# Two seams of a macaron block (FFN, attention, FFN): a low part ahead of the stage's last scaling, back-transposes behind two value units, and a last group finished and stored in halves

## The reference

```
x = x + 0.5 * ffn(layernorm(x))
x = x + attention(layernorm(x))      # q, k of width 16, v of width 64, 16 heads
x = x + 0.5 * ffn(layernorm(x))
```

## Time and profile before

| | us |
|---|---|
| median of 3 runs | 790.72 (789.14 to 791.90) |
| the profiled execution, its own time | 790.52 |
| its span, first to last instruction | 788.70 |
| PE busy, share of the span | 774.3, 98% |
| DVE busy, share of the span | 675.9, 86% |
| ACT busy, share of the span | 616.1, 78% |

### The profile page before, as it was taken

How to read it: one execution, slowest core, us unless ns; L and a number is a source line. 1 busy time by engine, 2 the same in 40 slices (tenths; PEclk the granted TensorE clock), 3 DMA queues, 4 the chain that set the end, 5 groups by cost and what they waited for, 6 DMA issues and landing times.

```text
span 788.7 us, 11788 instructions
## 1 busy us (share of the span) xinstructions
PE 774.3 (98%) x3638; PEld 467.5 (59%) x3638; DVE 675.9 (86%) x1347; ACT 616.1 (78%) x1018; POOL 201.6 (26%) x262
## 2 busy tenths in 40 slices
PE   8989999999999999999999999999999899999998
PEld 5868888888773333333333332333498678888886
DVE  6888878889869999999999999999547888878786
ACT  3867766766668999999999999999616676777763
POOL 3115633334301111111111112111112037333331
PEclk8999999999999999999999999999999999999999
DMA  6041312110274111111311111110000123202111
GB/s 178 1 164 53 108 54 107 53 54 1 107 289 139 54 54 53 55 54 54 107 54 54 54 54 54 54 54 1 2 1 1 48 117 141 73 20 87 54 53 54
DMA packets 25413, 54.65 MB, mean 69 GB/s; under 512 B 5264, under 2 KB 10768, under 8 KB 23312
## 3 DMA queue, kind: packets, MB, share of 16 engines
q1 hardware_dynamic: 25360, 54.00, 20.0%
HBM read 44.42 MB, written 9.57 MB: 68 GB/s over the span
## 4 chain that ended last, share of the span: by engine, by line
PE 90%; DVE 5%; ACT 2%; DMA 2%; issue 1%; SPq 0%; POOL 0%; DVEq 0%; ACTq 0%
PE ps L932 29%; PE ps L920 11%; PE ps L368 7%; PE ps L379 7%; PE ps L370 7%; PE ps L369 7%; PE ps L380 7%; PE ps L381 7%; PE ps L939 4%; ACT ef L1009 1%; PE ps L350 1%; DMA w2raw<-in_w 1%; DVE hlo L645 1%; PE ps L200 1%; DMA xt<-in_x 1%
## 5 line engine op out<-in xcount | busy, mean ns | idle before, releaser
L1073 DVE TENSOR_SCALAR_CACHE_REDUCE ef<-ps 128x1024 f32<-128x1024 f32 x256 | 307.2, 1214 | 6.6 <-PE ps L920 0.2
L1009 ACT ACTIVATE ef<-ef,nmax 128x1024 f32<-128x1024 f32 x256 | 293.9, 1149 | 8.9 <-DVE ef L1073 2.3
L932 PE MATMUL ps<-ef,vs 128*64 128x512 f32 x1024 | 247.9, 605 | 0.2
L454 ACT ACTIVATE ps<-ps,b_sb 128x512 f32<-128x512 f32 x256 | 169.0, 663 | 94.9 <-PE ps L370 92.9
L645 DVE TENSOR_TENSOR hlo<-ps,hhi 128x512 fp32r<-128x512 f32 x256 | 165.4, 685 | 4.5 <-ACT ps L454 0.2
L932 PEld LDWEIGHTS ps<-ef,vs 128*64 128x64 f32 x1024 | 62.7, 136 | 120.5 <-issue 108.2
L641 DVE CAST hhi<-ps 128x512 fp32r<-128x512 f32 x128 | 87.6, 684 | 54.2 <-ACT ps L454 54.1
L1117 POOL TENSOR_TENSOR vs<-V,rsum 128x128 f32<-128x128 f32 x128 | 51.3, 401 | 294.1 <-DVE rsum L1079 294.1
L501 POOL TENSOR_TENSOR acc<-acc,ysc 128x512 f32<-128x512 f32 x55 | 70.7, 1289 | 150.7 <-DVE ysc L668 150.1
L368 PE MATMUL ps<-xhi,w1lo 128*128 128x512 f32 x256 | 102.6, 401 | 0.4 <-DVE hlo L645 0.3
L379 PE MATMUL ps<-hhi,w2lo 128*128 128x512 f32 x256 | 101.5, 397 | 0.9 <-DVE gT L716 0.9
(11 more groups left out here) (98 smaller groups left out, 675.0 us busy)
## 6 DMA issues: line engine op xcount, KB each, us to landing
gb<-gates SPq DMA_DIRECT2D x16, 1024.0 KB, 4.6
qs<-qk_parts SPq DMA_DIRECT2D x32, 256.0 KB, 3.3
ks<-qk_parts SPq DMA_DIRECT2D x32, 256.0 KB, 3.9
w1raw<-in_w SPq DMA_DIRECT2D x16, 256.0 KB, 4.9
w2raw<-in_w SPq DMA_DIRECT2D x16, 256.0 KB, 5.6
qk_parts<-sthi SPq DMA_DIRECT2D x16, 256.0 KB, 2.3
qk_parts<-stlo SPq DMA_DIRECT2D x16, 256.0 KB, 2.9
xt<-in_x SPq DMA_DIRECT2D x4, 256.0 KB, 4.3
```

The source lines that it names most:

```text
L454: nc.scalar.activation(bank(mc), bank(mc), ACT.Gelu, bias=b1_sb[:, u, mc:mc + 1]).then_inc(F.gelu, 1)
L932: last = nc.tensor.matmul(bank(6 + half)[x * VD:(x + 1) * VD, :], vs[:, t % VRING, x * VD:(x + 1) * VD], ef[:, (2 * t + x) % ERING, half * ...
L1009: nc.scalar.activation(ef[:, c, :], ef[:, c, :], ACT.Exp, scale=-1.0, bias=nmax[:, c:c + 1], accum_out=esum[:, c:c + 1]).then_inc(s_exp, 1)
L1073: nc.vector.tensor_scalar(ef[:, c, :], bank(slot_bank(u), 2), -1.0, None, ALU.mult, ALU.min, accum_out=nmax[:, c:c + 1]).then_inc(s_max, 1)
```

## The change

At the first seam, VectorE runs `low_dve` of group 0 before the scaling of stage 7 and no longer after it. TensorE runs `back_pe` of group 3 after `values(0)` and `values(1)` and no longer between `queries(0)` and `values(0)`; `values(0)`, which writes bank 7, waits for one scaling fewer (that of stage 6, which reads this bank).

At the end, the scaling of the last stage is two instructions of 256 columns, each with a semaphore of its own; `finish_pe` writes tiles 0 and 1 to bank 1 and tiles 2 and 3 to bank 2 and waits for each half; the residual of group 3 is two instructions of 256 columns; and its store is two DMAs of 128 KB. VectorE's order there is both halves of the scaling, the residual of group 2, both halves of the last residual. Three semaphores are added.

```diff
+        def finish_bank(t):
+            return bank((1, 2)[t // 2])[:, t * P:(t + 1) * P]
+
         def finish_pe(pe, n, g):
             F = ffns[1]
             pe.wait_ge(F.acc, A0 + GR * (E - 3) + g + 1)
...
+            for half in range(2):
+                for t in range(2 * half, 2 * half + 2):
+                    at = (g * TPG + t) * P
+                    nc.tensor.matmul(finish_bank(t), acc[:, at:at + P], ident, start=True, stop=False)
+                    if t == 0:
+                        pe.wait_ge(s_part, 1)
+                    if t == 2:
+                        pe.wait_ge(F.scaled, S0 + GR * E)
+                    last = nc.tensor.matmul(finish_bank(t), ysc[:, (2 * GR - 1) % 2, t * P:(t + 1) * P],
+                                            ident, start=False, stop=True)
+                last.then_inc(s_fin, 1)
+
+        def last_scaled_dve(dve):
+            F, s = ffns[1], 2 * GR - 1
+            dve.wait_ge(F.y, (E // 2 - 1) * 2 * GR + (s + 1 + Y0))
+            dve.wait_ge(F.acc, (E // 2 - 1) * 2 * GR + (s + A0 - 1 - GR))
+            for half in range(2):
+                part = slice(half * 256, half * 256 + 256)
+                at = (GR - 1) * 512 + half * 256
+                nc.vector.scalar_tensor_tensor(ysc[:, s % 2, part], bank(Y_BANKS[s % 4])[:, part], b2_sb[:, E - 1:E],
+                                               gb[:, 1, at:at + 256], ALU.add,
+                                               ALU.mult).then_inc((s_part, F.scaled)[half], 1)
+
+        def last_residual_dve(dve, n):
+            g = GR - 1
+            for half in range(2):
+                dve.wait_ge(s_fin, half + 1)
+                at = g * TPG + 2 * half
+                xg = xt[:, at:at + 2, :]
+                src = bank((1, 2)[half])[:, half * 256:half * 256 + 256].rearrange("p (t d) -> p t d", d=D)
+                nc.vector.tensor_tensor(xg, xg, src, ALU.add).then_inc(s_last, 1)
...
+                residual_dve(dve, m, 1)
                 if m.k == 1:
-                    residual_dve(dve, m, 1)
+                    low_dve(dve, m, 0)
                     back(i, 7)
-                    low_dve(dve, m, 0)
                     statistics_dve(dve, m, 1)
                 else:
-                    residual_dve(dve, m, 1)
-                    back(i, 7)
+                    last_scaled_dve(dve)
                     residual_dve(dve, m, 2)
-                    residual_dve(dve, m, 3)
+                    last_residual_dve(dve, m)
...
                 if unit == 0:
-                    pe.wait_ge(ffns[0].scaled, S0 + GR * E)
+                    pe.wait_ge(ffns[0].scaled, S0 + GR * E - 1)
...
             queries(0)
-            back_pe(pe, n, 3)
             values(0)
             values(1)
+            back_pe(pe, n, 3)
...
-            for g in range(GR):
+            for g in range(GR - 1):
                 sp.wait_ge(norms[3].res, g + 1)
                 sp.dma_start(out_v[g], xt[:, g * TPG:(g + 1) * TPG, :]).then_inc(s_out, 16)
-            sp.wait_ge(s_out, 16 * GR)
+            for half in range(2):
+                sp.wait_ge(s_last, half + 1)
+                at = (GR - 1) * TPG + 2 * half
+                sp.dma_start(out_v[GR - 1][:, 2 * half:2 * half + 2, :], xt[:, at:at + 2, :]).then_inc(s_out, 16)
+            sp.wait_ge(s_out, 16 * (GR + 1))
```

More of the change, by code:

```diff
@@ L136, in macaron_kernel @@
         s_out = sem("s_out")
+        s_part = sem("s_part")
+        s_fin = sem("s_fin")
+        s_last = sem("s_last")
         class Norm:
```

## The result

The changed kernel has a median of 787.54 us in 22 runs (785.96 to 793.31), the kernel before 790.91 us in 22 runs (787.87 to 795.90); the ratio is 0.9958, with a 95% interval of 0.9942 to 0.9975. The profiled execution of the changed kernel took 788.84 us, its span is 787.0, with the same mean granted clock as the profiled one of before, 0.993: 1.7 us shorter. The mean granted clock is TensorE's, as a share of full speed over the whole execution. These two numbers, 3.4 us between the medians and 1.7 us between two executions at one clock, are what had to be explained.

What follows compares the result with a forecast made beforehand. TensorE held 90% of the chain that ended last, so only places where the chain leaves it could save. First seam 0.49 plus end 0.97 made 1.46 us, taking 790.72 to 789.3 us (0.18%), range 788.2 to 790.9.

Steps and rivals of the forecast that it cites:

- The seam's step of 0.49 us: First seam: TensorE starts 1.26 us early, but VectorE's chain lets 0.49 us remain; bounds 0 and 1.26.
- predicted wait of 1.0 to 1.4 us: First seam: TensorE's wait ahead of `forward_pe` of group 2 grows from 0.57 to about 1.3 us.
- The half instructions: End: a scaling of 256 columns takes 0.48 us, a residual of 256 columns 0.41 us.
- The end, put at 0.97: End: 0.97 us earlier, from 0.56 by the engines and 0.46 by the half store, less 0.05 lost.
- the prediction's own signs of being wrong: First scores not 0.49 us earlier, attention of another length, or span's end still 2.67 us behind the last issue.
- How the numbers follow: Prediction's section on cases and range: forecast 0.60, likeliest 789.3 us, range 788.2 to 790.9, within 0.3% at 0.86.
- the moved back-transposes: First seam: `back_pe` of group 3 comes at 204.6, after GpSimd's addition ending at 204.40, so no wait; no gain stated.
- The seam gives nothing: Rival, chance 0.15: another wait, nearest the keys' landing before the first scores, takes the first seam's gain; 789.75 us.
- The stores don't overlap: Rival, chance 0.05: at the end each store waits for the one before to land; slower, 792.0 us.
- The end gives little: Rival, chance 0.12: half instructions cost nearly the whole, or last byte's receipt doesn't follow the size; 789.9 us.
- the half store: End: the last store of 128 KB saves 0.46 us by the rows; the skill's rate gives an estimated 0.30.
- All of the lead stays: Rival, chance 0.06: first seam keeps all 1.26 us of TensorE's lead; with the end 2.2 us, 788.5 us.

Runs made afterwards that it cites:

- the low part alone: Kernel before with only the swap putting `low_dve` of group 0 ahead of the scaling: 792.72 us, ratio 0.9997; again 792.61 us, 0.9998.
- e11_change_third: The changed kernel run a third time, no edit, against the kernel before in the same rounds: median 788.44 us, ratio 0.9969.
- e2_change_again: The changed kernel run once more, no edit, against the kernel before in the same rounds: median 791.20 us, ratio 0.9981.
- e15_change_fourth: The changed kernel run again in later rounds, no edit, against the kernel before: median 789.56 us, ratio 0.9982.
- the seam alone: Kernel before with only the first seam's edits (low part, back-transposes, one scaling fewer to wait for): median 788.95 us, ratio 0.9978.
- the end alone: The changed kernel with the first seam's edits taken out, against the kernel before: median 789.96 us, ratio 0.9969.
- the filled kernel: Kernel before plus five matmuls that nothing reads, ahead of the first query unit at the first seam; first set 790.42 us, ratio 0.9977.

## Why the prediction came out as it did

**The sum held in its steps.** It said 1.46 us; at equal clock it is 1.65 (intervals 1.47 to 1.85 and 1.49 to 1.79 for the first set and the later three, 1.52 to 1.78 for all). The traces add up to 0.50 us to the first scores and 0.94 at the end, 1.44; the 0.2 us between that and the fit aren't explained. The low part at VectorE's idle time, no wait of `queries(0)`, `rstd` behind GpSimd's addition: each is in the trace where it was put. The seam's step of 0.49 us measured 0.54 at the forward transposes, and of TensorE's predicted wait of 1.0 to 1.4 us there 0.83 came at the transposes and 0.56 at `queries(3)`, which the prediction had named. The half instructions, put at 0.48 and 0.41 us, are 0.478 and 0.422. The end, put at 0.97, is 0.94 and 0.95 in traces and 1.06 (0.82 to 1.30) at equal clock. Of the prediction's own signs of being wrong, one showed in the profiled execution: the first scores came 0.33 us earlier and not 0.49, as the keys were waited for; over the traces of either kind it is 0.50.

**The step that failed is the one from the sum to the median**, in "How the numbers follow": "The runs spread over 789.14 to 791.90, so a median moves by some tenths of its own". This term was mis-sized: a median moves by over 3 us. The executions of one kernel differ in mean granted clock from 0.983 to 0.998, and 0.001 is worth 0.61 us, so they spread over 9 us; three runs had shown 2.8 of it. The first result compared 22 executions of the changed kernel at 0.9941 with 22 of the kernel before whose clocks aren't on record; their mean time, 791.31 us, fits 0.9925 (an estimate from the slope). The means of the two lists lie 791.31 - 788.65 = 2.66 us apart: 1.65 of the change and 1.0 of the 0.0016 between the clocks. The other 0.7 of the 3.4 us is where a median falls in a lopsided list: the changed kernel's is 1.11 us below its mean, with 14 of its 22 executions at 0.996 or 0.998, and that of the kernel before 0.40 below. So the measured 0.42% owes about half to which executions were drawn, and the forecast of 0.18% is near what the change itself does, 0.21%. A range from the sum and from the clock would have reached down to some 786.5 (787.91, the kernel before at 0.998, less 1.46). The 0.3% given as what can be told from no change was about right: the intervals of the ratios are 0.3 to 0.6% wide.

**A step without a price that was worth something.** The prediction gave the moved back-transposes a wait that they avoid, but no price: VectorE's chain was to bind whatever their place, as the expectation of the low part alone spells out (0.5 to 0.6 us without them). They bring 0.18 of the seam's 0.54 us. The part on VectorE was right: its chain runs equally early with and without them (9.37 and 9.38 us). What was left out is TensorE's own path. Standing 1.05 us for GpSimd's addition costs it most of its 1.26 us of lead, and from there its matmuls alone take until 211.89, 0.25 us beyond the end of VectorE's normed tiles. So with the low part alone TensorE binds, not VectorE.

**The rivals.** "The seam gives nothing", by the landing of the keys, is a real wait, but for a part and not in every execution: in the profiled one it took 0.2 us, in that of `e11_change_third` 0.5 (30.84 us to the first scores), in those of `e2_change_again`, `e15_change_fourth` and the seam alone next to none (30.34, 30.41 and 30.33), and it struck a trace of the kernel before as well (31.26 in place of 30.92). "The stores don't overlap" is refuted by the one burst of three stores. "The end gives little" is refuted by the end alone and by the run with one store; the half store is worth 0.41 us by its trace. By the rate of 436 GB/s in the Trainium skill (DMA: Bandwidth & Descriptors, Anatomy of one DMA), which that section gives for DMAs issued by GpSimd and not by SyncE as here, it was an estimated 0.30 us; the trace decides for more, and the fit over the clocks, 0.34, is too wide to choose. "All of the lead stays" is refuted by the wait of 0.40 us at the forward transposes.

**Theory B**, that TensorE's stand at the seam brings the clock down, looked good in the filled kernel (0.9934) and in the third run of the changed one (0.9938), at 12 runs a kernel, and found no support in the rounds where both kinds ran together (0.9922 beside 0.9925 and 0.9915).

## What to carry to other kernels

Before a change of a few tenths of a per cent is judged, look at the mean granted clock of every execution, and compare at equal clocks: here that made a difference of 0.2% plain (1.65 us, 1.52 to 1.78), with 0.41 us of scatter, where the medians of one and the same kernel lay 0.46% apart (787.54 and 791.20). Ahead of a prediction, look for stretches of low clock in the profile and ask whether each would come again; if not, the range must hold their price. And where one engine's chain is said to bind, work out the path of the engine that waits for it as well, with every stand left in it: here TensorE's own path was 0.25 us the longer one without the moved back-transposes, and a move without a price brought a third of the seam's gain.

## What the runs showed of the hardware that I had not expected

The granted clock of TensorE falls to half (1.2 GHz) for about 3 to 7 us after a stand, but in some executions only: at 240 and at 624 us in 8 of 15 traces, always both or neither. Ahead of these stretches TensorE stands at most 1.53 us at a time (1.53 and 0.45 us in the router, 0.95 and 0.59 at the attention's entry), so the "1.5 us and more" of one expectation doesn't describe the entry; the stand of 1.09 us at the first seam was followed by no low stretch in any trace. What sets these places apart isn't shown. The Trainium skill (TensorE: Matmul & The Clock Gate, Part 1: The HAM clock gate) says that the throttled state is the default and that activity releases it; the traces agree, as seven matmuls a router and five at the entry, whose results nothing reads, kept the clock up at these places in all three traces with them and brought the mean from 0.992 to 0.9957 (kernel before), 0.9978 and 0.9962 (changed). In the same rounds they took 2.0 us off the median of the kernel before (791.12 to 789.12, ratio 0.9975, 0.9959 to 0.9992), about as much as the change under study. For the changed kernel it is 1.2 us in the same rounds, which isn't clear of the noise; over all rounds its median went from 789.13 (36 executions at 0.9926) to 786.97 (14 at 0.9969).

The stretch at the start of the kernel wasn't touched and is in all 18 traces, but not always as long: over 9 to 21 us the granted clock is 0.57, 0.72 or 0.86. By itself that takes 0.002 to 0.007 off the mean over the kernel (an estimate: 12 us times what is lacking, over 787 us), and it is what the filled kernels' clocks still differ by in their traces: 0.995 with 0.72, 0.993 and 0.994 with 0.57.
